# Four attention layers on one core: the next batch's first maximum products begin beside the last quad of the second self-attention layer, and their shift is sent in the middle of the tail

## The reference

```
xn = rmsnorm(x, norm_w)
q = xn @ Wq;  k, v = encoder_out @ Wkv;  k_win, v_win = xn @ Wwin
linear_out = (q_phi @ kv_state) / (q_phi @ k_state + EPS_DEN)      # phi = 1, x, quadratic terms
scores = q @ k_win / sqrt(16);  allowed = (j <= i) & (j >= i - 64)
window_out = softmax(where(allowed, scores, min)) @ v_win
x = x + concatenate([linear_out, window_out]) @ Wout
```

## Time and profile before

| | |
|---|---|
| median of three executions | 2269.08 us (2267.74 to 2269.49) |
| profiled execution | 2270.52 us |
| span of the profile | 2268.7 us |
| TensorE (PE) busy | 2040.1 us, 90% |
| VectorE (DVE) busy | 1384.0 us, 61% |
| ScalarE (ACT) busy | 1146.9 us, 51% |
| GpSimd (POOL) busy | 749.1 us, 33% |
| mean granted TensorE clock | 0.965 of 2.4 GHz |

### The profile page before, as it was taken

How to read it: one execution, slowest core, us unless ns; L and a number is a source line. 1 busy time by engine, 2 the same in 40 slices (tenths; PEclk the granted TensorE clock), 3 DMA queues, 4 the chain that set the end, 5 groups by cost and what they waited for, 6 DMA issues and landing times. The chain is left out here.

```text
span 2268.7 us, 38499 instructions
## 1 busy us (share of the span) xinstructions
PE 2040.1 (90%) x14610; PEld 1341.6 (59%) x14610; DVE 1384.0 (61%) x3055; ACT 1146.9 (51%) x1755; POOL 749.1 (33%) x914
## 2 busy tenths in 40 slices
PE   4999999999998889997999898998999996989989
PEld 2333433343342268885565565756677775988989
DVE  5875776685767566645445454442687783756655
ACT  2256465555554766643536445263455454545444
POOL 3023124113213253322626336153110101646656
PEclk8799999999998999998999999999999997999999
DMA  6706304502530000027531707210422210000000
GB/s 149 133 11 119 47 6 76 87 8 52 94 74 1 1 15 1 10 72 112 122 54 54 122 7 140 52 61 15 158 85 97 76 38 1 8 12 13 15 12 20
DMA packets 77773, 126.67 MB, mean 56 GB/s; under 512 B 16650, under 2 KB 34826, under 8 KB 77582
## 3 DMA queue, kind: packets, MB, share of 16 engines
q1 hardware_dynamic: 74966, 122.63, 25.5%
q10 hardware_dynamic: 2624, 1.58, 0.2%
HBM read 93.59 MB, written 30.32 MB: 55 GB/s over the span
## 5 line engine op out<-in xcount | busy, mean ns | idle before, releaser
L1074 DVE TENSOR_REDUCE nmx_causal<-banks 128x1 f32<-128x333 f32 (+4 forms) x896 | 435.7, 538 | 178.5 <-PE banks L805 176.5
L963 ACT ACTIVATE probs_causal<-banks 128x1024 f32<-128x1024 f32 (+5 forms) x384 | 331.1, 899 | 263.3 <-PE banks L830 259.2
L805 PE MATMUL banks<-ks_causal,qs_causal 96*128 96x333 bf16 (+4 forms) x896 | 272.5, 340 | 14.0 <-DVE nmx_causal L1074 7.9
L728 POOL TENSOR_SCALAR_AFFINE_SELECT probs_window<-probs_window 128x512 f32<-128x512 f32 (+1 forms) x272 | 162.2, 604 | 276.6 <-ACT probs_window L963 265.9
L728 POOL TENSOR_SCALAR_AFFINE_SELECT probs_causal<-probs_causal 128x512 f32<-128x512 f32 (+2 forms) x160 | 92.9, 581 | 459.3 <-ACT probs_causal L963 459.0
L830 PE MATMUL banks<-qs_causal,ks_causal 97*128 97x512 bf16 (+5 forms) x896 | 211.6, 331 | 21.2 <-ACT probs_causal L963 15.6
L1074 DVE TENSOR_REDUCE nmx_window<-banks 128x2 f32<-128x384 f32 (+2 forms) x320 | 140.9, 460 | 105.7 <-PE banks L805 103.1
L854 PE MATMUL banks<-probs_causal,v_causal 128*17 128x512 f32 (+5 forms) x1792 | 187.5, 492 | 0.0
L803 PEld LDWEIGHTS banks<-below,identb 128*128 128x128 bf16 x512 | 49.6, 98 | 173.2 <-DVE nmx_causal L1074 124.6
L963 ACT ACTIVATE probs_window<-banks 128x768 f32<-128x768 f32 (+2 forms) x128 | 99.7, 785 | 102.8 <-PE banks L830 102.7
L805 PEld LDWEIGHTS banks<-ks_causal,qs_causal 96*128 96x128 bf16 x896 | 86.8, 100 | 105.3 <-DVE nmx_causal L1074 61.6
(11 more groups left out here) (256 smaller groups left out, 4142.9 us busy)
## 6 DMA issues: line engine op xcount, KB each, us to landing
fs_masked<-in_fside SPq DMA_DIRECT2D x32, 616.0 KB, 3.7
ks_causal<-zk SPq DMA_DIRECT2D x96, 137.6 KB
ks_window<-zk SPq DMA_DIRECT2D x96, 137.6 KB
qs_causal<-zq SPq DMA_DIRECT2D x96, 128.0 KB
qs_window<-zq SPq DMA_DIRECT2D x96, 128.0 KB
zk<-parts_causal SPq DMA_DIRECT2D x24, 275.2 KB, 2.8
zk<-parts_window SPq DMA_DIRECT2D x24, 275.2 KB, 2.4
zq<-parts_causal SPq DMA_DIRECT2D x24, 256.0 KB, 7.3
```

Source lines behind the costliest of these rows:

```text
L728: pool.affine_select(out=v, in_=v, compare_op=ALU.is_ge, fill=0.0, base=const, pattern=[[0, QH], [by_c, wd]], channel_multiplier=by_p).the ...
L805: ins = pe.matmul(bk[:, c:c + m], qs[q][0:KR, h, t * P:(t + 1) * P], ks[q][0:KR, h, key:key + m], start=cover is None, stop=True, skip_gro ...
L963: ins = act.activation(dst, src, ACT.Exp, scale=DH ** -0.5)
L1074: dve.tensor_reduce(dst, src, AX.X, ALU.max, negate=True).then_inc(emptied_v, 1)
```

## The change

For batches 0 to 2 of the window layer, the 20 maximum products of the next batch are no longer spread over the tail. They are spread from the middle of quad 3 to the middle of the tail, and the shift stands directly behind the last of them, eight tokens before the end of the tail instead of five.

```diff
         if not first:
             tail = [t for i in range(NT + 1) for t in ([("mix", b, i)] * (i < NT) + [("out", b, i - 1)] * (i > 0))]
+            batch += tail
             if b + 1 < B:
-                tail = spread(tail, ring_tokens(b + 1, 0, ring_jobs), 0, len(tail) - AHEAD + 1)
-                tail.insert(len(tail) - AHEAD + 3, ("shift", b + 1, 0))
-            batch += tail
+
+                end = len(batch) - len(tail) // 2
+                batch = spread(batch, ring_tokens(b + 1, 0, ring_jobs), ends[2] + (ends[3] - ends[2]) // 2, end)
+                batch.insert(end + len(ring_jobs) * QH, ("shift", b + 1, 0))
```

## The result

| | before | after |
|---|---|---|
| median | 2269.08 us (7 executions, 2261.93 to 2273.57) | 2250.85 us (7 executions, 2246.46 to 2259.98) |
| profiled execution | 2270.52 us | 2246.87 us |
| span | 2268.7 us | 2245.1 us |
| TensorE busy | 2040.1 us | 2021.6 us |
| mean granted clock | 0.965 | 0.972 |

The ratio is 0.9929 (95% interval 0.991 to 0.9947), faster by 16.1 us (12.0 to 20.4); the two medians lie 18.2 us apart. The forecast was 2254.4 us, 14.6 us faster. Single executions of either kernel differ by more than 10 us, so the rest is read from traces.

A forecast was written before the change was run, and what follows sets the result against it. TensorE, busy 90% of the span, bounds the kernel. Three passages (-10.7 us) and the clock (-3.9) make -14.6: from 2270.5 to 2255.9, forecast as 2254.4 us against the median 1.4 us lower; range 2250.5 to 2263.0.

The forecast's parts named there:

- Part 1: Second half of quad 3: thirteen maximum products (3.39 us of TensorE) move in, and the first mix comes only 1.81 us later.
- Part 2: Tail, from the first mix to the next batch's first scores: 21.00 us in place of 26.38.
- Part 3: Shift directly behind the last product in the tail: its transpose waits 0.83 us for VectorE's minimum, all on the path.
- Per passage: Each of three batch passages: first mix 1.81 us later, tail 5.38 us shorter, together -3.57 us.
- Part 4: Passages of batches 1 and 2: denser work keeps the clock up, both falls go, -3.94 us (bounds 0 and 3.94).
- 1 (clock still falls): Rival: products fill the waits, but the clock still falls at two passages, by phase; 2258.4 us, chance 0.24.
- 2: Rival: filling is half paid back by delayed scores, later ScalarE and banks less often free; 2263.8 us, chance 0.13.
- 3: Rival: quad 3's products push the chain by their full 3.39 us, plus the shift's wait; 2271.6 us, chance 0.07.
- 4 (clock falls in the tail behind the new wait): Rival: low clock behind the shift's wait adds 5.1 us per passage, today's falls kept; 2273.7 us, chance 0.04.
- 5: Rival, faster still: batch 2's 2.62 us wait of quad 3's scores for a shift also goes; 2251.8 us, chance 0.02.

## Why the prediction was right

**Part 1, thirteen products in quad 3.** Predicted: scores 1.70 us later, waits of 0.68, 0.47 and 0.76 us, first mix 1.81 us later. Measured in batch 0: from the scores before the first product (1145.29) to the last scores 6.30 us against 4.80 (the record before at 1142.60, then 1147.40), so 1.50 later; waits of 0.64, 0.36 and 0.76; first mix 1.59 us later (12.92 against 11.33). None is worse than forecast, and the first mix comes 0.2 us earlier than forecast, which is won in the first step. Most of that can be read in these rows of the kernel before:

```profile
1142.60 0.49 PE L830 MATMUL banks<-qs_window,ks_window 97*128 97x192 bf16 x4
1143.03 0.62 PE L854 MATMUL banks<-probs_window,v_window 77*17 77x256 f32 x8
1143.58 0.51 PE L830 MATMUL banks<-qs_window,ks_window 97*128 97x192 bf16 x4
...
1146.95 0.13 PEld L854 LDWEIGHTS banks<-probs_window,v_window 128*17 128x17 f32 x8 [0.28 <-POOL probs_window L728]
```

The wait of 0.39 us costs 0.47 from start to start (from scores to values 0.90, 1143.58 to 1144.48, in place of 0.43), and the values at 1146.95 waited about 0.08 us for GpSimd's mask; the products took up both, and neither was in the sum. With useless products in nearly the same places, and the old tail behind them, the same 3.39 us of work cost 1.76 us at the first mix (27.20 against 25.44).

**Part 2, the tail.** 21.00 predicted, 21.01 measured. Walking the tokens with starts of the earlier trace rows and the wait for a bank of the ring where one is due gave the tail to a hundredth; the errors of the single steps (out 0 at 1.62, the shift 0.04 us late) cancelled.

**Part 3, the added wait.** 0.83 predicted from the distance in the earlier trace rows, 0.76 measured. It is on the path, but taking it away gave 0.52 back, not the whole 0.83: here the size was too high.

**Per passage** -3.57 predicted, -3.78 measured, three of them -11.3 us.

**Part 4, the clock.** -3.94 us for two falls predicted. At the quad's end and in the tail the clock fell in neither trace of the changed kernel, and the reason given for it, density, is now shown by adding useless work. (In the second trace it fell in the first half of batch 2's quad 3, behind the wait of 2.91 us, where the change adds nothing.) What the prediction had not seen is that the falls of the trace it read were a draw: over all sparse ends 18 of 26 fall. In batches 0 to 2 it is 10 of 14, about two per execution, at some 1 to 2 us each and at a few more, so the term was about right on average by luck. With -11.3 it makes -15.3 us, inside the measured 12.0 to 20.4.

**Rivals.** 1 (clock still falls) fell, with no fall at the quad ends and in the tails of the changed kernel's six passages and 1 in 24 with its variants; 2 and 3 (filling paid back, chain pushed by its full length) fell with the first mix 1.6 us later for 3.39 us of work; 4 (clock falls in the tail behind the new wait) did not occur in any trace. 5 took the wait of 2.62 us for an event of one execution that might go. It is one, but another comes: in the two traces of the changed kernel quad 3's scores waited up to 1.72 and 2.91 us.

## What to carry to other kernels

Work that is ready early is worth most in the last waits of the section before, and what it costs is only the part that stands ahead of the instruction which releases the next wait: count that part, token by token. Look at the granted clock at places with several short waits in a row, since filling them may pay twice, and even useless matmuls may be free there. Before bringing a load forward or back, look at the DMA share of the stretch that it moves to.

## What the runs showed of the hardware that was not expected

- The clock fell at 18 of 26 sparse quad ends, though at 17 of these 18 no single wait there exceeded 1.19 us, and at 1 of 24 with 3.4 us of additional matmul work in some 12 us. At a passage a fall cost 1.0 us with 3.4 us of low clock (52.75 against 51.80) and 2.0 with 6.8 (53.85 against 51.82), in batch 3 3.4 with 10.2 (48.7 against 45.3).
- The clock also fell in the first half of quad 3, in nine of the fourteen traces, the changed kernel's second among them. Each time it fell behind a wait of 1.25 us or more for the shift's landing; behind four others of 1.2 to 1.7 us it did not.
- The shift's DMA of 8 KB, sent by ScalarE, lands in 1.8 us on free queues. Behind the load of a stack the longest landing of each of twelve traces was 4.3 to 7.2 us, and quad 3's scores waited for it up to 3.8 us, most often in batch 2; with that load sent later the longest was 3.5 and 2.9. Such a wait with the low clock behind it put off the first mix of a passage by 6 to 7 us (33.11 against 27.03 us behind the transpose in the changed kernel, 34.37 against 27.69 in the one spread from the quad's start), so it may be a part of why executions of one kernel lie over 10 us apart; that was not shown.
- TensorE stopped in the middle of a token without a releaser in four of fourteen traces: for 1.48 and 2.85 us with the DMA share above 1, and for 0.49 and 0.76 us as a load ran out and just behind one.
